# Experts of a decoder kernel: rounds of three tiles with bias products, against an unrolled pipeline over single tiles with biases in the copies

## The reference

```python
gate_weights = jax.nn.softmax(jnp.einsum('bsd,dn->bsn', x, Wg) + bg, axis=-1)
topv, topi = jax.lax.top_k(gate_weights, 2)
h = gelu(jnp.einsum('bsd,ndh->nbsh', x, W1) + b1[:, None, None, :])     # 256 -> 512, exact gelu
h = gelu(jnp.einsum('nbsh,nhf->nbsf', h, W2) + b2[:, None, None, :])    # 512 -> 512
eo = jnp.einsum('nbsf,nfd->nbsd', h, W3) + b3[:, None, None, :]         # 512 -> 256
out = jnp.einsum('nbsd,bsn->bsd', eo, comb)                             # 8 experts, the best 2 of each token
```

## Time and profile before

| what | value |
|---|---|
| median of 3 runs | 1903.18 us (1901.72 to 1915.38) |
| profiled execution, its time | 1906.83 us |
| its span in the trace | 1905.0 us |
| mean granted TensorE clock | 0.923 |
| PE, PEld busy | 1466.9 us (77%), 879.7 us (46%) |
| DVE, ACT, POOL busy | 994.8 us (52%), 569.4 us (30%), 366.6 us (19%) |
| experts stage, PE busy in it | 346.0 us, 339.2 us |
| routing stage, PE busy in it | 62.0 us, 0.4 us |

### The profile page before, as it was taken

One profiled execution on the slowest core, in us unless ns is written; L12 is line 12 of the kernel. 1 busy time (PEld: TensorE's weight loads), 2 busy tenths in 40 slices (PEclk: granted clock), 3 DMA queues, 4 the chain that ended last, 5 costly groups with the idle time before them and its releaser, 6 DMA issues. The chain is left out here.

```text
span 1905.0 us, 29364 instructions
## 1 busy us (share of the span) xinstructions
PE 1466.9 (77%) x9284; PEld 879.7 (46%) x9409; DVE 994.8 (52%) x2728; ACT 569.4 (30%) x1154; POOL 366.6 (19%) x499
## 2 busy tenths in 40 slices
PE   2368878777878777219999999448888887699997
PEld 1134444444444443106556655235555554366664
DVE  6156666665666653302222222337877864367775
ACT  0123333343433333001111111224555554223231
POOL 2121112121112110140000000335554440000000
PEclk9979999999999997659999999567998998699999
DMA  3522322223322320560011110264443431200000
GB/s 110 200 49 54 52 46 49 45 48 56 52 47 47 47 41 13 197 220 22 28 33 33 33 33 16 74 155 104 112 113 100 101 85 31 75 1 12 12 1 23
DMA packets 173965, 122.41 MB, mean 64 GB/s; under 512 B 33387, under 2 KB 163571, under 8 KB 173873
## 3 DMA queue, kind: packets, MB, share of 16 engines
q1 hardware_dynamic: 158032, 102.41, 22.7%
q10 hardware_dynamic: 12768, 10.49, 1.7%
q0 software_dynamic: 3072, 8.39, 1.5%
HBM read 47.54 MB, written 21.76 MB: 36 GB/s over the span
## 5 line engine op out<-in xcount | busy, mean ns | idle before, releaser
L936 ACT ACTIVATE first_probs<-pair 128x512 f32<-128x512 f32 x320 | 177.5, 595 | 132.1 <-PE pair L435 129.1
L476 DVE TENSOR_REDUCE first_negmax_x<-bank 128x2 f32<-128x512 f32 x256 | 168.7, 684 | 61.7 <-PE bank L420 54.9
L435 PE MATMUL pair<-kept_stack_cross 98*128 98x256 bf16 x768 | 152.5, 282 | 10.8 <-ACT first_probs L936 6.7
L420 PE MATMUL bank<-kept_stack_cross 96*128 96x256 bf16 x768 | 156.9, 288 | 3.4 <-issue 1.7
L1831 ACT ACTIVATE second_probs<-pair 128x512 f32<-128x512 f32 x192 | 113.7, 597 | 126.7 <-PE pair L435 124.0
L1383 PE MATMUL pair<-kept_w,experts_hidden_t 128*128 x416 | 142.6, 486 | 0.0
L413 PE MATMUL bank<-kept_mask_q,kept_ident 128*128 128x512 bf16 x232 | 92.9, 401 | 56.8 <-DMA kept_stack_cross<-first_parts_x_q 30.6
L476 DVE TENSOR_REDUCE second_negmax_x<-bank 128x2 f32<-128x512 f32 x128 | 88.5, 692 | 59.4 <-PE bank L420 51.8
L420 PEld LDWEIGHTS bank<-kept_stack_cross 96*128 96x128 bf16 x768 | 77.5, 104 | 63.9 <-issue 24.7
L1964 POOL DMA_INDIRECT second_routed<-expert_out,kept_slots x32 | 32.6, 1019 | 360.7 <-POOLq L105 353.1
L1383 PEld LDWEIGHTS pair<-kept_w,experts_hidden_t 128*128 128x128 f32 x416 | 77.0, 190 | 51.1 <-issue 45.9
(11 more groups left out here) (426 smaller groups left out, 2959.5 us busy)
## 6 DMA issues: line engine op xcount, KB each, us to landing
kept_stack_self<-first_parts_a SPq DMA_DIRECT2D x128, 64.0 KB, 3.1
kept_w<-in_L_ffn_W SPq DMA_DIRECT2D x8, 1024.0 KB, 15.2
kept_stack_self<-second_parts_a SPq DMA_DIRECT2D x128, 64.0 KB, 2.9
kept_stack_cross<-first_parts_x_k SPq DMA_DIRECT2D x96, 64.0 KB
kept_stack_cross<-first_parts_x_q SPq DMA_DIRECT2D x96, 64.0 KB
kept_stack_cross<-second_parts_x_k SPq DMA_DIRECT2D x96, 64.0 KB, 2.6
kept_stack_cross<-second_parts_x_q SPq DMA_DIRECT2D x96, 64.0 KB
experts_expert_rows<-by_expert SPq DMA_DIRECT2D x39, 128.0 KB, 2.0
```

Of the source, the lines that this page charges most:

```text
L420: mm = pe.matmul(out, q, k, start=mask is None, stop=True, skip_group_check=True)
L435: mm = pe.matmul(out, k, q, start=mask is None, stop=True, skip_group_check=True)
L476: return dve.tensor_reduce(negmax[:, 2 * n:2 * n + 2], bank[:, :].rearrange("p (m t) -> p m t", t=D), AX.X, ALU.max, negate=True)
L936: act.activation(probs[(phase + n) % PROBS][:, :], key_bank[n % KEYBANKS][:, :], ACT.Exp, scale=att.scale).then_inc(probs_made, 1)
```

## The change

**Preparation.** The loads, the three-way split, the clearing and the laying of `bias` are gone.

**Routing.** ACT issues three DMAs at the start: b1 and b2 as 8 rows of 1024 into `b_raw`, and b3 (8x256) broadcast to all 128 partitions (1 MB in SBUF). PE turns `b_raw` in eight pieces into `b12`, a column for each expert and block of 128 features; it stands ahead of the two counting products. ACT copies it out ahead of its two exponentials.

**Experts.** The loop is written out over 39 tiles. In step n, PE makes the first layer of tile n, the second of tile n-1, turns the first hidden tile of n, makes the third layer of n-2, turns the second hidden tile of n-1, and turns the rows of tile n+1. The bias products are gone. DVE now copies the raw layer out of PSUM before it is turned, and ACT applies the gelu after the turn, in four pieces of 128x128, each with a bias column picked by the expert's register. DVE adds b3 as it copies the result. PE, ACT and DVE each load the owner of each tile to a register.

**Second layer.** The numbers of its schedule get names, and two slots in which nothing is done fall away at the ends. Its instructions keep their order.

```diff
 def prepare_weights(nc, d, t, ps):
-        for w, n in (("L0_ffn_b1", FH), ("L0_ffn_b2", FH), ("L0_ffn_b3", D)):
-            loads.append((b_raw[:, at:at + n], d[w]))
-            at += n
...
-            sp.wait_ge(bias_cleared, 1)
-            sp.wait_ge(bias_split, 1)
-            for part in range(3):
-                sp.dma_start(t["bias"][part:part + 1, :, :], b_parts[:, part, :]).then_inc(bias_laid, 16)
...
-            pool.memset(t["bias"][:, :, :].bitcast(F32), 0.0).then_inc(bias_cleared, 1)
...
-            dve.tensor_copy(b_parts[:, 0, :], b_raw[:, :])
-            dve.drain()
-            dve.tensor_tensor(b_rest[:, :], b_raw[:, :], b_parts[:, 0, :], ALU.subtract)
...
 def route_tokens(nc, d, t, ps):
         @block.tensor
         def _(pe):
+            pe.wait_ge(b12_loaded, 32)
+            for k in range(2 * FH // P):
+                mm = pe.transpose(ps[2][:, k * NE:(k + 1) * NE], b_raw[:, k * P:(k + 1) * P], t["ident"][0:NE, 0:NE])
+            mm.then_inc(b12_turned, 1)
             pe.wait_ge(chosen_made, 1)
...
         @block.scalar
         def _(act):
+            for n, w in enumerate(("L0_ffn_b1", "L0_ffn_b2")):
+                act.dma_start(b_raw[:, n * FH:(n + 1) * FH], d[w]).then_inc(b12_loaded, 16)
+            act.dma_start(t["b3"][:, :, :].rearrange("p e f -> p (e f)"), d["L0_ffn_b3"].rearrange("e f -> (e f)").partition_broadcast(P)).then_inc(b3_loaded, 16)
+            act.wait_ge(b12_turned, 1)
+            act.activation(t["b12"][:, :, :].rearrange("p k e -> p (k e)"), ps[2][:, 0:2 * FH // P * NE], ACT.Copy)
             act.wait_ge(less_made, 1)
...
 def run_experts(nc, d, t, ps):
+            def turn_rows(n):
+                pe.wait_ge(rows_loaded[n % U], 16 * (n // U + 1))
+                if n >= 1:
+                    pe.wait_ge(rows_copied, n)
                 for j in range(KT):
-                    mm = pe.transpose(turn_bank[u][:, j * P:(j + 1) * P], rows[u][:, j * P:(j + 1) * P], ident[:, :])
+                    mm = pe.transpose(rows_bank[:, j * P:(j + 1) * P], rows[n % U][:, j * P:(j + 1) * P], ident[:, :])
                 mm.then_inc(rows_turned, 1)
...
+            def first_layer(n, expert):
+                pe.wait_ge(rows_copied, n + 1)
+                if n >= 1:
+                    pe.wait_ge(h1_kept, n)
+                for k in range(KT):
+                    mm = pe.matmul(layer1_bank[:, :], rows_t[n % 2][:, k, :], t["w1"][:, bass.ds(expert, 1), k, :].rearrange("p a f -> p (a f)"),
+                                   start=(k == 0), stop=(k == KT - 1))
+                mm.then_inc(h1_made, 1)
...
+            turn_rows(0)
+            for n in range(TILES + 2):
+                if n < TILES:
+                    experts[n] = pe.value_load(t["owner"][0:1, n:n + 1], min_val=0, max_val=NE - 1)
+                    first_layer(n, experts[n])
+                if 1 <= n <= TILES:
+                    second_layer(n - 1, experts[n - 1])
+                if n < TILES:
+                    turn_first(n)
+                if n >= 2:
+                    third_layer(n - 2, experts[n - 2])
+                if 1 <= n <= TILES:
+                    turn_second(n - 1)
+                if n + 1 < TILES:
+                    turn_rows(n + 1)
...
+            def second_gelu(n, expert):
+                act.wait_ge(h2_turned, n + 1)
+                if n >= 2:
+                    act.wait_ge(out_made, n - 1)
+                for k in range(4):
+                    ins = act.activation(hidden2_t[n % 2][:, k, :], turn2_bank[:, k * P:(k + 1) * P], ACT.Gelu, bias=t["b12"][:, 4 + k, bass.ds(expert, 1)])
+                ins.then_inc(h2_done, 1)
...
+            copy_rows(0)
+            for n in range(TILES + 2):
+                if n < TILES:
+                    keep_first(n)
+                if 1 <= n <= TILES:
+                    keep_second(n - 1)
+                if n >= 2:
+                    finish(n - 2)
+                if n + 1 < TILES:
+                    copy_rows(n + 1)
```

More of the change, by code:

```diff
@@ L1318, in run_experts @@
         sb, sem = open_tensors(nc, ctx, "experts")
-        rows = [sb(f"expert_rows_{u}", [P, D]) for u in range(3)]
-        rows_t = [sb(f"expert_rows_t_{u}", [P, KT, P]) for u in range(3)]
-        hidden = [sb(f"hidden_{u}", [P, FH]) for u in range(3)]
-        hidden_t = [sb(f"hidden_t_{u}", [P, 4, P]) for u in range(3)]
-        done = [sb(f"expert_done_{u}", [P, D]) for u in range(3)]
-        U = 3
-        turn_bank = [ps[0], ps[1], ps[2]]
-        layer_bank = [ps[3], ps[4], ps[5]]
+        U = 3
@@ L1354, in _, with store @@
+            def store(n):
+                sp.wait_ge(out_copied, n + 1)
+                sp.dma_start(d["expert_out"][n * P:(n + 1) * P, :], done[n % U][:, :]).then_inc(stored[n % U], 16)
+            for n in range(U):
+                load(n)
+            for n in range(TILES):
+                if n + U < TILES:
+                    load(n + U)
+                store(n)
             for u in range(U):
-                sp.wait_ge(stored[u], 16 * (ROUNDS + 1))
+                sp.wait_ge(stored[u], 16 * (TILES // U))
@@ L1402, in _, with turn_first @@
[L1402 to L1413 removed]
+            def turn_first(n):
+                pe.wait_ge(h1_kept, n + 1)
+                if n >= 1:
+                    pe.wait_ge(h1_done, n)
+                for j in range(4):
+                    mm = pe.transpose(turn1_bank[:, j * P:(j + 1) * P], hidden1[n % 2][:, j * P:(j + 1) * P], ident[:, :])
+                mm.then_inc(h1_turned, 1)
@@ new lines, in second_layer, with third_layer @@
+            def second_layer(n, expert):
+                pe.wait_ge(h1_done, n + 1)
+                if n >= 1:
+                    pe.wait_ge(h2_kept, n)
+                for k in range(4):
+                    mm = pe.matmul(layer2_bank[:, :], hidden1_t[n % 2][:, k, :], t["w2"][:, bass.ds(expert, 1), k, :].rearrange("p a f -> p (a f)"),
+                                   start=(k == 0), stop=(k == 3))
+                mm.then_inc(h2_made, 1)
+            def third_layer(n, expert):
+                pe.wait_ge(h2_done, n + 1)
+                if n >= 1:
+                    pe.wait_ge(out_copied, n)
+                for k in range(4):
+                    mm = pe.matmul(layer3_bank[:, 0:D], hidden2_t[n % 2][:, k, :], t["w3"][:, bass.ds(expert, 1), k, :].rearrange("p a f -> p (a f)"),
+                                   start=(k == 0), stop=(k == 3))
+                mm.then_inc(out_made, 1)
@@ new lines, in _ @@
+            experts = {}
+            turn_rows(0)
[13 more added lines that the diff above has]
+                    turn_rows(n + 1)
@@ L1417, in _, with first_gelu @@
             act.preload_act_table(ACT.Gelu)
-            with act.Fori(0, ROUNDS) as i:
-                for u in range(U):
-                    act.wait_ge(h1_made, U * i + u + 1)
-                    act.activation(hidden[u][:, :], layer_bank[u][:, :], ACT.Gelu).then_inc(h1_done, 1)
-                for u in range(U):
-                    act.wait_ge(h2_made, U * i + u + 1)
-                    act.activation(hidden[u][:, :], layer_bank[u][:, :], ACT.Gelu).then_inc(h2_done, 1)
+            def first_gelu(n, expert):
+                act.wait_ge(h1_turned, n + 1)
+                if n >= 2:
+                    act.wait_ge(h2_made, n - 1)
+                for k in range(4):
+                    ins = act.activation(hidden1_t[n % 2][:, k, :], turn1_bank[:, k * P:(k + 1) * P], ACT.Gelu, bias=t["b12"][:, k, bass.ds(expert, 1)])
+                ins.then_inc(h1_done, 1)
@@ L1446, in _, with copy_rows, keep_first @@
-            for u in range(U):
-                copy_rows(0, u)
-            with dve.Fori(0, ROUNDS - 1) as i:
-                copies(i, False)
-            copies(ROUNDS - 1, True)
+            def copy_rows(n):
+                dve.wait_ge(rows_turned, n + 1)
+                if n >= 2:
+                    dve.wait_ge(h1_made, n - 1)
+                dve.tensor_copy(rows_t[n % 2][:, :, :].rearrange("p j q -> p (j q)"), rows_bank[:, 0:D]).then_inc(rows_copied, 1)
+            def keep_first(n):
+                dve.wait_ge(h1_made, n + 1)
+                if n >= 2:
+                    dve.wait_ge(h1_turned, n - 1)
+                dve.tensor_copy(hidden1[n % 2][:, :], layer1_bank[:, :]).then_inc(h1_kept, 1)
```

306 lines of the change are left out of this document (136 added, 170 removed).

## The result

| | before | after |
|---|---|---|
| median of the runs | 1906.22 us (1901.72 to 1915.68) | 1917.88 us (1911.29 to 1926.33) |
| ratio to before, 95% interval | 1 | 1.0057 (1.0038 to 1.0076) |
| profiled execution, span | 1905.0 us | 1915.6 us |

The changed kernel is slower by 0.57%, which is 10.9 us of 1906.2 (7.2 to 14.5). That is inside the 1% which the prediction called no change. Its median of 1917.9 is 5 us above the forecast of 1913; 3 of these come from the kernel before, whose median is 1906.2 here and was 1903.2 in the three runs that the forecast started from. The two profiled spans differ by 10.6 us.

The account below looks back on a forecast made before the run. PE was taken to bound the experts, at 8.64 us a tile. Experts +13.2, routing +1.5 and preparation -4.4 summed to +10.3 us, on the median of 1903.2 giving 1913.5, rounded 1913, with a range of 1893 to 1934.

Parts of the forecast that it names:

- Bias products: Experts on PE: dropping them saves 0.54 us a tile over 39 tiles, 21 us, all on the path.
- Row turn and first layer: Each experts step's end: PE stands still 0.8 us (0.6 to 1.1) until DVE has copied the turned rows.
- The owner's register: Experts: PE's 0.8 us load is off the path; without its cover it would cost 0.6 to 0.8 us a tile.
- Weight loads: Experts, third layer right behind turns: its float32 weight load costs 0.1 us a tile (0 to 0.2).
- The other waits: Experts steps: second turn's wait for DVE's copy has slack 1.2 us; second layer's wait for the gelu is hidden.
- Ends of the pipeline: Experts' first and last steps: with 10.5 us from the steps, they make the stage 13.2 us longer.
- Preparation, -4.4: Before the first layer: bias loads and DVE work go, next stage starts at 38.4 instead of 42.75 us (-3 to -6).
- Routing, +1.5: Routing: b1 and b2 must land before ACT's exponentials, moving DVE's chain to the scatters by 0 to 3 us.
- Second layer and retrieval, 0: Stages after the experts: only two empty slots go from the second layer, so 0 us; retrieval also 0.
- (a): Rival, experts: the row turn's wait is hidden or nearly, 31 us come back, 1882 us; chance 0.10.
- (b): Rival, experts: stops make the clock give way; 1930 us at 0.95, 1965 at 0.86; chance 0.13.
- (c): Rival, experts: a second wait opens in each step, 12 us per 0.3, 1925 for the first 0.3; chance 0.12.

Follow-up runs that it names:

- experiment 1: Changed kernel with PE's turn of the next tile's rows ahead of the third layer and DVE's copy ahead of the result's addition: 1883.83 us, ratio 0.9876.
- Experiment 6: Changed kernel with the first layer's two waits placed ahead of PE's load of the owner's number: 1939.24 us, ratio 1.0167.
- 7: Changed kernel with an extra DVE copy of the turned rows into a spare tile, ahead of the one PE waits for: 1928.39 us, ratio 1.0106.
- Experiment 2: Kernel before without the experts' bias products, those biases left out of the result: 1887.53 us, ratio 0.9882.
- Experiment 9: Kernel before with the expert loops of PE, ACT, DVE and SP written out as straight code: 1912.13 us, ratio 1.0022.
- experiment 4: Changed kernel with PE's turns of b1 and b2 behind the counting products and ACT's copy behind the exponentials: 1912.58 us, ratio 1.0027.
- experiment 5: Changed kernel with the row turn and its copy earlier, and the turns and copy of b1 and b2 later: 1878.28 us, ratio 0.9846.
- 8: Changed kernel with the old bias preparation put back into a tile nothing reads, b3 placed elsewhere: 1924.89 us, ratio 1.0081.
- 3: Kernel before without the experts' bias products and without the preparation of the bias tile, biases left out: 1888.05 us, ratio 0.9886.

## Why the prediction was right

**Right in substance.** The forecast was +10.3, the measurement +10.9 with an interval of 7.2 to 14.5. That the two agree so closely is luck. The stages that the change touches gave +5.5: the experts' term was 4.9 too high, routing's 0.8 too low and the preparation gave 0.7 more. What brings the total back to +10.9 is 5 us for which the sum had no term.

*What bounds.* PE in the experts, and what it waits there counts in full: experiments 1, 6 and 7 moved the stage by their step's change times the number of steps (-31.7, +25.4 and +13.0 us).

*Bias products, 21 us.* Experiment 2 gave 19.9 on the stage. Right.

*Row turn and first layer, 0.8 a tile.* The handover was built as 0.38 + 0.03 + 0.41 + 0.20 = 1.02 and measured 0.38 + 0.04 + 0.42 + 0.14 = 0.98, so the stop is 0.76. But 0.09 of the first layer's slot belongs to it, and its whole cost is 0.86 (experiment 1). The place, the releaser and the strictness were right. The release of 0.20 was read wrongly: it took a third of the 1.89 of three copies for the first one's end. But these copies overlap, and one lasts 0.68 on the mean, so the first ended near 963.28 and the product followed at 963.43, 0.15 later there as well.

```profile
L1435 DVE COPY experts_hidden_t<-bank 128x512 f32<-128x512 f32 x39 | 24.5, 683 | 78.9 <-PE bank L1372 78.9
```

*The owner's register, hidden, 0.6 to 0.8 without cover.* Experiment 6: hidden, and 0.65 without.

*Weight loads, 0.1 behind the turns.* Wrong: the slot from the turn to the third layer is 0.43, no longer than before. A similar 0.09 appeared behind the stop, where I had none. The step came out at 8.83 for 8.91.

*The other waits.* None in a steady step; the two waits for DVE's copies at the start (0.78 and 0.35) and the one for ACT at the end (1.40) are in the first and last steps, as the ends' terms had them.

*Ends of the pipeline, stage +13.2.* The mis-sized term: the stage is +8.3. From the first product to the end of the last third layer it was to take 352.8, and took 348.6. Of that 3.7 are the steps: 326.0 for 37, where the sum had 329.7. One of the 3.7 is a slip in the sum: it charged the stop to all 37, but the last of them (1177.37 to 1185.22, 7.85 us) has no rows to turn; the other 36 took 8.84 each for 8.91. Another 0.6 is the last step, whose wait for the gelus was shorter than built. Further, the first product comes 3.5 us after the stage's start, for 6.3 before, 0.9 more gained than charged.

```profile
844.23 0.66 PE L1350 MATMUL bank<-kept_ident,experts_expert_rows 128*128 128x128 f32 x2 [57.77 <-DMA experts_expert_rows<-by_expert]
845.50 3.78 PE L1374 MATMUL bank<-kept_w,experts_expert_rows_t 128*128 x4 [0.61 <-DVE experts_expert_rows_t L1447]
850.06 0.66 PE L1358 MATMUL bank<-kept_ident,experts_hidden 128*128 128x128 f32 x4 [0.78 <-DVE experts_hidden L1453]
```

```profile
1192.39 1.97 PE L1392 MATMUL pair<-kept_w,experts_hidden_t 128*128 x8 [1.40 <-ACT experts_hidden_t L1430]
```

*The loop, 0.* Experiment 9: nothing at the border, 0.6 us on the stage's rounds, and a total that the runs don't tell from before.

*Preparation, -4.4.* -5.1, and SP's own list was what came late next, as said.

*Routing, +1.5.* +2.3. Its cause, ACT's exponentials behind b1 and b2, is shown by experiment 4. The prediction took 5.3 us for a small landing under load, but that row is of a transfer of 128 KB; b1 and b2, 16 KB each, took 5.7 from the start of their issue. The first scatter was put near 796.5 and stands at 796.6, since the earlier start (-5.0 for -4.4) and the longer wait (+2.3 for +1.5) nearly cancel.

*Second layer and retrieval, 0.* They are 5.0 us longer in the profiled execution, with the same instructions. SP issues the last load of a tile 297 us into the stage in both kernels; the difference comes in the last 50 us, where the clock was granted differently, 0.81 before and 0.70 after.

```profile
1592.20:1641.20 49.00, 29.20 (x199) 15.54 (x197) 15.92 (x40) 14.80 (x32) 2.20 (x4) 0.81 0.08 18
```

```profile
1597.70:1650.20 52.50, 33.98 (x196) 17.33 (x195) 15.78 (x39) 15.11 (x32) 2.19 (x5) 0.70 0.07 17
```

Over all profiles the second layer's stage ran from 445 to 458 us, in the old order of the experts (449.1, 458.4, 448.1, 453.7) as in the new one, so nothing shows a cost of the change there. The retrieval took 263.8 to 264.6 us in the four profiles with the old order and 264.3 to 265.4 in the seven with the new one: some 0.9 of its 1.6 may belong to the change, and nothing here shows how.

**The rivals.** (a), the wait hidden, came true only in experiments 1 and 5, where the turn was moved; the changed kernel as it is has it in full. (b), the clock giving way: not in the steady part, which had 1.00 from 880 to 1185, with PE busy for 0.93 of the time. The second failure mode that the Trainium skill describes (TensorE: Matmul & The Clock Gate, A second HAM failure mode), short idles between groups of products that make the clock fall and rise again, did not show there, with a stop of 0.76 in each 8.83 us. (c), a second wait: none.

**What stays open.** The changed stages of the profiled pair give +5.5, the median +10.9 with 7.2 as its lower end. A part may lie at the start of the experts, where the new order works in short pieces between stops. In five profiles with the new order (after, 1, 5, 6, 7) PE got its full clock during the first tile; in the other two (4 and 8) only some ten us later, and their experts stages were 359.4 and 358.6 for 355.7. The same stretch, first in the changed kernel, then in 4: PE is as busy, at another clock, and gets through fewer passes (15 for 21).

```profile
846.00:856.00 10.00, 8.61 (x21) 3.38 (x20) 1.80 (x3) 1.14 (x4) 0.00 (x0) 0.84 0.04 11
```

```profile
850.80:860.80 10.00, 8.61 (x15) 3.55 (x15) 1.12 (x2) 1.14 (x4) 0.00 (x0) 0.50 0.04 12
```

In the old order, where PE works through the first round without a stop, none of the four profiles (before, 2, 3 and 9) has it: the first tile's passes are slow and those of the second at full clock. That would be 3 to 4 us in some executions. Two of seven against none of four is too little to call it shown, and what is left of the 5 us I can't name. The other kernels say that it need not belong to the change: a kernel's ratio, in us, less what the three stages show in its profile, is +5.4 here, but -0.4 in experiment 5 and -1.5 in 4, which have the same change but for an order, and +5.9 in 9, which has nothing of it but the loop. Over all ten it runs from -2.7 to +5.9, with intervals of 4 to 8 us to each side.

## What to carry to other kernels

When a pipeline is written out tile by tile, look at what each step ends with: an operation whose result has to go through another engine before the next step can begin costs the whole handover (here 0.86 us, 32 us over the stage) and can eat a gain that was bought elsewhere (here 20 us). Moving it ahead of work that doesn't need it is two pieces of code in another order; with it the kernel is 1.2% faster than the one before instead of 0.6% slower, and 1.5% with the biases' turns out of the routing's way, of which last step only the routing stage shows the gain.

A load or a copy that is needed later shouldn't be put ahead of what the next engine waits for: b1 and b2 were not needed for another 60 us, and cost 2.3.

Compare two profiles stage by stage, and take only the stages that the change touches as evidence: those with the same instructions differ by up to 12 us from one execution to the next, more than this change is worth.

## What the runs showed of the hardware that I had not expected

- Stages with the same instructions took 736.7 to 749.1 us (first layer) and 445.4 to 458.4 us (second layer) in eleven profiles. Where I looked, PE's busy time and the clock granted differed with it: 29.2 us at 0.81 and 34.0 us at 0.70 at the end of the second layer.
- Two DVE copies of 128x256 from PSUM, each 0.41 to 0.42 us in its record, start 0.34 apart when they follow each other: the record's duration is more than what a second one costs.
- A first layer of four passes takes 1.72 us when it follows other products, and 1.81 when PE has stood still for its tile. Its first weight load starts 0.10 us ahead of the first product in the one case and together with it in the other; that this is the 0.09 is my reading.
- PE goes on 0.14 us after the end of the DVE copy that releases it, and 0.79 when a register must be loaded in between.
